# One-tile units in the stage that sums neighbours a second time and runs the dense experts

## The reference

```python
def _graph_conv(x, W, b, edge_src, edge_dst, edge_weight, num_nodes):
    support = x @ W
    msgs = support[edge_src] * edge_weight[:, None]
    agg = jax.ops.segment_sum(msgs, edge_dst, num_segments=num_nodes)
    return agg + b
h = jax.nn.relu(_graph_conv(x, W1, b1, ...))          # first aggregation
x = x + _graph_conv(h, W2, b2, ...)                   # second aggregation
# mixture of 6 experts on layernorm(x), all computed for every node
rh = relu(f @ router_w1 + router_b1); logits = softmax(rh @ router_w2 + router_b2)
top_w, top_i = top_k(logits, 2); routing_weights = softmax(top_w)
h1 = relu(f @ w1[e] + b1[e]); h2 = relu(h1 @ w2[e] + b2[e]); out_e = h2 @ w3[e] + b3[e]
x = x + sum over the two chosen e of routing_weight * out_e
# then z = mish(layernorm(x) @ W_dense.T + b_dense) for the edge layer that follows
```

## Time and profile before

| | us |
|---|---|
| median of 3 runs | 4284.08 |
| lowest and highest run | 4277.53, 4288.81 |
| span of the profiled execution | 4272.1 |
| PE busy in the span | 3514.0 (82%) |
| DVE busy | 2295.0 (54%) |
| ACT busy | 1939.7 (45%) |
| POOL busy | 2823.4 (66%) |

### The profile page before, as it was taken

The page is one execution under the profiler, slowest core; times in us unless marked ns, Lnnn a source line. Parts: engine busy times, 40 slices in busy tenths (PEclk is TensorE's granted clock), DMA queues, the critical chain, the costliest instruction groups (busy, mean ns, idle before and its releaser), DMA issues. The chain is left out here.

```text
span 4272.1 us, 68475 instructions
## 1 busy us (share of the span) xinstructions
PE 3514.0 (82%) x17723; PEld 3093.3 (72%) x17723; DVE 2295.0 (54%) x6976; ACT 1939.7 (45%) x3024; POOL 2823.4 (66%) x2732
## 2 busy tenths in 40 slices
PE   4777777777756899999999968888888888649999
PEld 4666666666645788888888867777777777538887
DVE  6566556556554445545445436666666666632222
ACT  4455555555541333333333445555555555423333
POOL 3677777777767777766676227777777777353444
PEclk7788788888776999999999987777777787559999
DMA  6455555555543222222222126666666666534443
GB/s 177 154 187 188 179 174 183 178 180 178 178 140 107 69 68 66 69 66 64 68 67 64 36 96 208 212 206 212 209 209 208 212 211 191 172 137 92 98 98 60
DMA packets 287817, 605.53 MB, mean 142 GB/s; under 512 B 61999, under 2 KB 163342, under 8 KB 287499
## 3 DMA queue, kind: packets, MB, share of 16 engines
q1 hardware_dynamic: 166267, 344.34, 25.0%
q0 software_dynamic: 114784, 245.67, 21.0%
q10 hardware_dynamic: 6576, 13.36, 0.9%
HBM read 460.33 MB, written 144.67 MB: 142 GB/s over the span
## 5 line engine op out<-in xcount | busy, mean ns | idle before, releaser
L1669 POOL DMA_INDIRECT y_node<-node_table,src_sb x832 | 847.6, 1019 | 379.2 <-issue 378.9
L509 POOL DMA_INDIRECT conv_gath<-support_table,src_sb x832 | 878.4, 1056 | 284.3 <-issue 259.9
L1110 POOL DMA_INDIRECT x_gath<-hidden_table,src_sb x832 | 792.9, 953 | 353.6 <-issue 259.9
L664 PE MATMUL conv_pz<-conv_we,conv_edge 128*128 128x256 f32 x2240 | 643.1, 451 | 76.9 <-PEq L97 76.7
L1682 PE MATMUL y_pa<-y_hot,y_node 128*128 128x64 f32 x3328 | 523.6, 326 | 181.7 <-PEq L97 181.1
L1682 PEld LDWEIGHTS y_pa<-y_hot,y_node 128*128 128x128 f32 x3328 | 506.8, 240 | 214.7 <-issue 212.0
L664 PEld LDWEIGHTS conv_pz<-conv_we,conv_edge 128*128 128x128 f32 x2240 | 510.2, 234 | 170.2 <-issue 81.4
L655 PE MATMUL conv_ps<-conv_hot,conv_gath 128*128 128x64 f32 x1664 | 255.6, 305 | 213.5 <-DMA conv_gath<-support_table,src_sb 210.9
L655 PEld LDWEIGHTS conv_ps<-conv_hot,conv_gath 128*128 128x128 f32 x1664 | 242.5, 219 | 245.9 <-DMA conv_gath<-support_table,src_sb 238.5
L1734 ACT ACTIVATE y_node<-y_node 128x1024 f32<-128x1024 f32 x208 | 219.4, 1056 | 340.6 <-ACTq L97 340.1
L1692 PE MATMUL y_pz<-y_we,y_edge 128*128 128x256 f32 x1104 | 361.0, 499 | 13.0 <-PEq L97 13.0
(11 more groups left out here) (256 smaller groups left out, 5844.8 us busy)
## 6 DMA issues: line engine op xcount, KB each, us to landing
conv_edge<-in_edge_t SPq DMA_DIRECT2D x140, 512.0 KB
edge_mish_table<-conv_neg SPq DMA_DIRECT2D x140, 512.0 KB
y_neg<-edge_mish_table SPq DMA_DIRECT2D x139, 512.0 KB, 4.2
y_edge<-in_edge_t SPq DMA_DIRECT2D x69, 512.0 KB
e_rows<-expert_rows SPq DMA_DIRECT2D x56, 272.0 KB, 3.3
conv_gath<-support_table,src_sb POOLq DMA_INDIRECT x832
x_gath<-hidden_table,src_sb POOLq DMA_INDIRECT x832
y_node<-node_table,src_sb POOLq DMA_INDIRECT x832, 3.1
```

The source lines that it names most:

```text
L509: pool.indirect_dma_start(gath[g % SLOTS][:, j, :], None, table[:, :], bass.IndirectOffsetOnAxis(ap=c.src[:, col:col + 1], axis=0),).then_ ...
L664: last = pe.matmul(ps_z[r % 2][:, j, :], edge[r][:, m, j * P:(j + 1) * P], we[:, m, :], start=m == 0, stop=m == KD - 1)
L1110: pool.indirect_dma_start(gath[g % SLOTS][:, j, :], None, table[:, :], bass.IndirectOffsetOnAxis(ap=c.src[:, col:col + 1], axis=0),).then_ ...
L1669: pool.indirect_dma_start(node[g % SLOTS][:, j, :], None, c.t3[:, :], bass.IndirectOffsetOnAxis(ap=c.src[:, col:col + 1], axis=0),).then_i ...
```

## The change

`PARTS` becomes 49 units of one tile. Nothing else is edited; `DUE`, the spread of the groups over the steps, the number of steps, the widths of the matmuls and activations, the loads and the stores follow from it. The buffers keep their sizes. In units 0 to 45 the groups now fall one each into steps 1, 2, 4 and 5, and a fifth into step 3 in every fourth unit; before, a pair had eight or nine over six steps.

```diff
-PARTS = (1, 1) + (2,) * 22 + (1, 1, 1)
+PARTS = (1,) * NT
 PARTS = tuple((sum(PARTS[:u]), n) for u, n in enumerate(PARTS))
 DUE = tuple(min(GROUPS, -(-E * (t + n) // (N * CG)) + SLACK) for t, n in PARTS)
```

## The result

The changed kernel takes 4505 us (median of 4, 4492 to 4515) against 4281 of the kernel before: ratio 1.0524, 95% interval 1.0506 to 1.0542. The forecast was 4499, slower. The span of the profiled execution grew from 4272.1 to 4512.7, by 240.6 us, and it grew where it was expected; the changed kernel's profiled execution, 4514.8 us, is the slowest of its four, 10 us above their median.

The account below looks back on a forecast made before the run. PE bounds the pairs; in one-tile units DVE's chain to the transposes makes PE wait. 1110.4 + 9.2 (fifth segments) + 158.6 + 36 = 1314 against 1099.3, 215 us more; span 4272.1 becomes 4487, median 4499 us, range 4365 to 4575.

Parts of the forecast that it names:

- PE's own work: PE's matmul work per tile in the stage: hardly changes when pairs become single units, taken as nothing.
- The base: Time of a one-tile unit without DVE's extra work: 24.14 us, 1110.4 us for 46 units.
- Gathers: POOL's gathers for a one-tile unit: 21.5 us, below 23.9, so no bound; near the start they help.
- The chain, 10.19 us: From a unit's origin (first layer of expert 1) to the next unit's transposes, through DVE and ACT: 10.19 us.
- One-hots and loads, 158.6 us, by step: Extra work in DVE's queue: 62.2 us in step 1, 54.8 in step 5, 41.6 in step 4.
- Taking nothing for steps 2 and 3: One-hots and loads in steps 2 and 3 cost nothing, as DVE waits for PE there; without that cover 78 us.
- The clock, 36 us: Slow PE clock after long waits at the transposes in 23 units: half of the upper bound of 72 us.
- Where PE waits: At the transposes of L988 in nearly every unit: some 1 us, 3 to 4 where step 1 has extras.
- Rival A: The chain shrinks below PE's work in one-tile units and PE keeps the pace: faster, say 4250 us; chance 0.05.

Follow-up runs that it names:

- hots_23_places_3: Changed one-tile kernel with one-hots built in steps 2 and 3 and the loads of places moved to step 3; 4332 us, ratio 1.0130 to the kernel before.
- pairs_halved: Kernel before, still in pairs, with the experts' first and second layers cut into one-tile matmuls and activations; 4284 us, ratio 1.0016.
- refine_first: Changed one-tile kernel with DVE's Mish finished after the moments, shares after the refinement, and next unit's transposes before the shares; 4436 us, ratio 1.0370 to the kernel before.
- hots_1: Changed one-tile kernel with every set of one-hots built in step 1, between moments and refinement; 4619 us, ratio 1.0805 to the kernel before.
- hots_23: Changed one-tile kernel with each set of one-hots built in the next step 2 or 3; 4428 us, ratio 1.0355 to the kernel before.

## Why the prediction was right

- **PE's own work: nothing.** Nearly right. At a clock of 1.00 (hots_23_places_3) PE is busy 1076.55 us for the 46 tiles, against 1052.82 at 0.98 before: at least 24 us more, of which pairs_halved, with 14, shows a part. The base was worked out from rows of one-tile units and so had it in.
- **Gathers: no bound, a gain at the start.** Right. POOL's idle time in the stage is now mostly for slots that DVE frees late (362 us from origin to origin, 94 before). Tile 4's origin is at 1459.1 in the changed kernel and at 1472.0 in the one before, 13 us earlier; then the longer units eat it up.
- **The chain, 10.19 us.** Right in its parts (7.65 against 7.71, 1.18 against 1.18) and as what PE waits for: refine_first shortened it by 1.1 to 1.8 us and gained 1.5 us per unit, about half of it clock. The base of 24.14 us is not seen in the changed kernel, whose shortest unit takes 25.1 us, since step 5 of the unit before often makes DVE late; in hots_23_places_3, with one-hots and loads out of the way, many units take 24.4 to 24.9.
- **One-hots and loads, 158.6 us, by step.** Right in kind: hots_1 and hots_23 differ by 192 us with the same instructions, and moving both gives 174. With the clock, 158.6 + 36 = 195 was the forecast of that. Taking nothing for steps 2 and 3 was nearly right: in hots_23_places_3, where they hold all sets and loads, units of four groups with one set in these steps take 23.0 to 25.0 us and those with two 24.4 to 26.0; the eight with two sets and a fifth group take 25.7 to 28.8.
- **The clock, 36 us: too small.** This is the term that was mis-sized. From changed kernel to hots_23_places_3 PE's busy time falls by 76.7 us with the same passes while the clock goes from 0.93 to 1.00, about the upper bound of 72 and twice what I took. I had counted the 23 units with an extra in step 1 at 3.15 us each or half of them; in the trace all 23 lie below 1.00, and 13 of the other 23 too. A unit at 0.94 loses some 1.5 us of PE's busy time, one at 0.89 some 2.8. What the Trainium skill describes (TensorE: Matmul & The Clock Gate, on HAM oscillation) was nearer than my half. The rest came out smaller: 236 - 77 = 159 us in place of 215 - 36 = 179.
- **Where PE waits.** I named L988, with 3 to 4 us where step 1 has an extra and some 1 us elsewhere. Where step 1 has one the wait is split between L1162 and L988, in the order of PE's queue; elsewhere it is 2.05 us (median), twice what I said, since DVE comes late from the steps before.
- **Rival A fell.** The rule of the Trainium skill (Perfetto Trace Analysis, Optimizing Scalar/DVE Operations), that breaking up instructions may let work be completed sooner where engines are not saturated but hold up others, does not carry here: DVE is busy 47% of the time, and its queue between the Mish and the last refinement, mostly operations of 0.16 us each that start 0.31 apart, got shorter by 18% with the tiles (9.33 to 7.65 us), PE's cover by 42%.

The sum came out within 6 us of the measured time, and that is partly luck. In the stretch it was short by 21 us (215 against 236): the clock was short by 41, and the rest gave back 20. The span as a whole was short by 26. What hides this is that the profiled execution lies 10 us above its median, and that I put the median 12.0 us above the span, while this execution lies only 2.1 above its own.

## What to carry to other kernels

Halving a unit takes away more of the work that covers a latency than of the latency (here 42% against 18%): add up, on the in-order queue of the engine in between, everything that stands between the producer and the consumer, related or not, and compare it with the cover that the smaller unit leaves. Work that recurs by another count than the unit's (here every third and sixth group) is cheap only where its engine waits anyway; moving it there was worth three quarters of the loss, the clock included, and moving it past the point where its result is due cost 120 us in the pairs.

## What was not expected of the hardware

The granted clock fell after waits none of which is longer than those that the kernel before bore at a clock of 0.99: after 1.40 and 2.05 us with one transpose between them it was 0.55, mostly 1.2 GHz, for 3.62 us (window above), while after a single 2.05 us, at 1877.52, the unit shows 1.00. Moving one kind of extra out of the chain brought the mean of the stretch back from 0.93 to 0.96 or 0.94, moving both to 1.00. In the kernel before the fall that I had used as a price came after 3.79 us.
